# Two value tiles of the 32-wide attentions projected inside heads 2 and 3

## The reference

```
q, k, v = split_heads(src @ w + b)            # 16 heads, 512 tokens, 32 wide
scores = einsum('bhqd,bhkd->bhqk', q, k) / sqrt(32)
scores = scores * mask - 10000.0 * (1.0 - mask)
out = einsum('bhqk,bhkd->bhqd', softmax(scores), v)
```

## Time and profile before

| | |
|---|---|
| median of 3 runs | 4309.42 us (4300.68 to 4310.7) |
| the profiled execution | 4298.77 us |
| its span in the trace | 4296.9 us |
| busy, share of the span | PE 88%, PEld 54%, DVE 61%, ACT 53%, POOL 39% |
| mean granted clock of PE | 0.955 |

### The profile page before, as it was taken

One profiled execution on the slowest core, in us unless ns is written; L12 is line 12 of the kernel. 1 busy time (PEld: TensorE's weight loads), 2 busy tenths in 40 slices (PEclk: granted clock), 3 DMA queues, 4 the chain that ended last, 5 costly groups with the idle time before them and its releaser, 6 DMA issues. The chain is left out here.

```text
span 4296.9 us, 65250 instructions
## 1 busy us (share of the span) xinstructions
PE 3771.7 (88%) x23680; PEld 2331.9 (54%) x23680; DVE 2631.9 (61%) x5803; ACT 2290.6 (53%) x4528; POOL 1696.6 (39%) x1869
## 2 busy tenths in 40 slices
PE   7889899898888989989888898998988898899898
PEld 4544565556544456555654545655555454555555
DVE  5765645656576564665657656466666775646655
ACT  5665734434666573444466657344446575634444
POOL 4544542232454454222245444422224644442222
PEclk9999999899999999989999999999998999999899
DMA  4042220102204221010220322201022132210102
GB/s 134 15 120 55 83 69 31 59 21 99 74 16 120 58 80 69 31 59 25 94 74 22 113 64 74 69 31 59 30 95 71 40 91 65 83 59 31 59 32 97
DMA packets 94554, 276.01 MB, mean 64 GB/s; under 512 B 25472, under 2 KB 25984, under 8 KB 73088
## 3 DMA queue, kind: packets, MB, share of 16 engines
q1 hardware_dynamic: 94208, 271.58, 19.7%
HBM read 201.24 MB, written 4.19 MB: 48 GB/s over the span
## 5 line engine op out<-in xcount | busy, mean ns | idle before, releaser
L806 POOL TENSOR_SCALAR probs<-probs,row_inv 128x512 f32<-128x512 f32 x1024 | 696.0, 697 | 638.8 <-DVE row_inv L721 638.8
L665 ACT ACTIVATE probs<-probs,row_max 128x512 f32<-128x512 f32 x1024 | 733.5, 725 | 130.2 <-DVE row_max L737 128.9
L560 PE MATMUL ps<-ident,probs 128*128 128x128 f32 x4096 | 609.7, 290 | 172.8 <-ACT pT L659 146.3
L560 PEld LDWEIGHTS ps<-ident,probs 128*128 128x128 f32 x4096 | 480.1, 147 | 383.6 <-ACT pT L659 210.1
L659 ACT ACTIVATE pT<-ps 128x512 f32<-128x512 f32 x768 | 430.5, 603 | 112.4 <-PE ps L560 111.5
L370 PE MATMUL ps<-mix,wring 128*128 128x512 f32 x1024 | 471.0, 596 | 3.1 <-DMA wring<-in_blocks_dram 3.1
L535 PE MATMUL ps<-kstack,qstack 96*128 96x512 f32 (+1 forms) x1024 | 381.0, 467 | 15.8 <-DVE row_max L737 6.5
L737 DVE CUSTOM_DVE_ANT_0 probs<-ps,maskA 128x512 f32<-128x512 f32 x512 | 329.2, 681 | 42.5 <-PE ps L535 42.5
L737 DVE CUSTOM_DVE_ANT_0 probs<-ps,neg 128x512 f32<-128x512 f32 x512 | 340.7, 685 | 8.9
L370 PEld LDWEIGHTS ps<-mix,wring 128*128 128x128 f32 x1024 | 191.2, 190 | 198.1 <-issue 178.6
L1550 POOL TENSOR_TENSOR hinv<-hvar,minus_half 128x32 f32<-128x32 f32 x24 | 146.3, 6094 | 284.4 <-DVE hvar L1260 284.4
(11 more groups left out here) (179 smaller groups left out, 7313.7 us busy)
## 6 DMA issues: line engine op xcount, KB each, us to landing
wring<-in_blocks_dram SPq DMA_DIRECT2D x151, 1024.0 KB, 5.1
qstack<-hi SPq DMA_DIRECT2D x256, 64.0 KB, 2.0
kstack<-hi SPq DMA_DIRECT2D x256, 64.0 KB, 2.0
maskA<-in_mask_dram SPq DMA_DIRECT2D x9, 1024.0 KB, 7.5
rows<-in_rows_dram SPq DMA_DIRECT2D x8, 1024.0 KB, 4.7
qstack<-hi SPq DMA_DIRECT2D x256, 32.0 KB, 2.0
qstack<-lo SPq DMA_DIRECT2D x128, 64.0 KB, 2.0
kstack<-lo SPq DMA_DIRECT2D x128, 64.0 KB, 2.0
```

The costliest lines, as they stand in the source:

```text
L560: ins = nc.tensor.transpose(tile[:, qc * P:(qc + 1) * P], probs[:, m % PSLOTS, qc, kc * P:(kc + 1) * P], ident[:, :])
L665: nc.scalar.activation(p, p, ACT.Exp, bias=row_max[:, n % PSLOTS, qc:qc + 1], scale=-1.0, accum_out=row_sum[:, n % PSLOTS, qc:qc + 1]).the ...
L806: nc.gpsimd.tensor_scalar(p, p, row_inv[:, (n - 1) % PSLOTS, qc:qc + 1], 1.0, ALU.mult, ALU.mult)\
```

## The change

The new list `projects` says which half projections stand in which head of attentions 1 and 2. The q and k tiles of groups 2 and 3 stay in heads 0, 1, 4 and 5. Value tiles 2 and 3 leave their place ahead of head 0 and are projected in heads 2 and 3, in two halves of two feature chunks each. DVE empties them after its last maximum of that head. Value tiles 0 and 1 stay ahead of the heads. In attention 2 nothing is left between the q tiles and head 0. `pe_values` becomes `pe_v` for one tile or half of one; attention 0 is computed as before. ACT's and POOL's conditions are written with `projects` and give the same instructions as before.

```diff
-        def to_N(pe, tile, w, src, tc, n=H, base_=0, fin=None, ready=None):
+        def to_N(pe, tile, w, src, tc, n=H, base_=0, fin=None, ready=None, fcs=range(C)):
-            for fc in range(C):
+            for fc in fcs:
...
+            if C - 1 in fcs:
+                m.then_inc(*fin)
...
+                self.projects = {0: ('q', 2), 1: ('k', 2), 2: ('v', 2), 3: ('v', 3), 4: ('q', 3), 5: ('k', 3)}
+                if self.shared:
+                    self.projects = {}
...
+        def pe_v(pe, A, tc, fcs=range(C), tile=None):
+            if tc == 0 and 0 in fcs:
+                w_wait(pe, A.vblk)
+            tile = take(pe, 'v', A.tag, tc) if tile is None else tile
+            to_N(pe, tile, weights(A.vblk), A.src, tc, n=A.vcols, base_=A.voff, fcs=fcs,
+                 fin=tile_ready.reach('v', A.tag, tc) if C - 1 in fcs else None)
+            return tile
...
             if t == 1:
...
                 pe_k(pe, A, 1)
-                pe_values(pe, A)
+                pe_v(pe, A, 0)
+                pe_v(pe, A, 1)
             if t == 2:
                 pe_queries(pe, A)
-                pe_values(pe, A, (2, 3))
...
-                    if not A.shared and g + 2 < A.groups and i < 2:
-                        part = (pe_q, pe_k)[i](pe, A, g + 2, fcs=(2 * half, 2 * half + 1), tile=None if half == 0 else part)
+                    if n in A.projects:
+                        kind, c = A.projects[n]
+                        part = {'q': pe_q, 'k': pe_k, 'v': pe_v}[kind](pe, A, c, fcs=(2 * half, 2 * half + 1),
+                                                                       tile=None if half == 0 else part)
...
         def dve_attention(dve, A):
             t = A.tag
             if t < 2:
-                dve_values(dve, A, range(C))
+                dve_values(dve, A, range(C) if A.shared else range(2))
...
                     if n < A.heads:
                         add_max(n, 2 * half + 1)
+                if A.projects.get(n, 'q')[0] == 'v':
+                    dve_values(dve, A, (A.projects[n][1],))
...
-                    dve_values(dve, A2, range(C))
+                    dve_values(dve, A2, range(2))
```

More of the change, by code:

```diff
@@ L380, in to_N @@
                 m = nc.tensor.matmul(tile[:, 0:n], src[:, fc, tc * P:(tc + 1) * P],
-                                     w[:, fc * H + base_:fc * H + base_ + n], start=(fc == 0), stop=(fc == C - 1))
-            m.then_inc(*fin)
+                                     w[:, fc * H + base_:fc * H + base_ + n], start=(fc == 0), stop=(fc == C - 1),
+                                     skip_group_check=(len(fcs) < C))
+            if C - 1 in fcs:
+                m.then_inc(*fin)
         def dve_stats(dve, tag, tc):
@@ L504, in pe_attention @@
                 pe_queries(pe, A, (0,))
-                pe_values(pe, A)
+                for tc in range(C):
+                    pe_v(pe, A, tc)
                 pe_queries(pe, A, (1, 2, 3))
@@ L675, in act_attention @@
                     nc.scalar.activation(oT[:, c, :], ps[:, OBANK, :], ACT.Copy).then_inc(*act_done.reach('context', t, c))
-                for step in (('x0', 'e0', 'x1', 'e2', 'x2', 'x3') if A.shared else ('e0', 'e1', 'x0', 'x1', 'e2', 'e3', 'x2', 'x3', 's')):
-                    if step == 's' and not A.shared and g + 2 < A.groups and i < 2:
-                        act_split(act, A, 'qk'[i], g + 2)
+                for step in (('x0', 'e0', 'x1', 'e2', 'x2', 'x3', 's') if A.shared else ('e0', 'e1', 'x0', 'x1', 'e2', 'e3', 'x2', 'x3', 's')):
+                    if step == 's' and A.projects.get(n, 'v')[0] != 'v':
+                        act_split(act, A, *A.projects[n])
                     if step[0] == 'e' and 0 <= m < A.heads:
@@ L689, in dve_values @@
             t = A.tag
-            if t < 2:
+            if t < 2 and 0 in tiles:
                 dve.wait_ge(sems['rows_in'], 16 * (t + 1))
@@ L797, in pool_attention @@
                 g, i = divmod(n - 1, 4)
[L798 to L802, removed]
+                if A.projects.get(n - 2, 'v')[0] != 'v':
+                    pool_split(pool, A, *A.projects[n - 2])
                 for qc in range(C):
@@ L1613, in _ @@
                     pe_k(pe, A2, 1)
-                    pe_values(pe, A2, (0, 1))
+                    pe_v(pe, A2, 0)
+                    pe_v(pe, A2, 1)
                     pe_norm_turn(pe, 'ln2', xn)
```

## The result

The changed kernel takes 4347.51 us (median of 4 runs), the kernel before 4308.39: the ratio is 1.0087, with a 95% interval of 1.0072 to 1.0102. It is slower by 0.9%. The forecast was +34 us, the measured difference of the medians +39.

A forecast was written before the change was run, and what follows sets the result against it. DVE's mask and maximum bound the heads, PE only in heads that also project; start gain, clock and stretch sum to +2.35 us in attention 1, +6.2 in attention 2, +34.2 over four samples: 4343 us, range 4317 to 4363.

The forecast's parts named there:

- The start: Ahead of head 0: attention 1 gains 3.35 us (3.0 to 3.8), until its last stack DMA lands; attention 2 gains 0.
- The stretch: Heads 2 to 5: moved value matmuls and evictions delay masks by 4.2 us per attention (bounds 1.2 to 6.7).
- The walk: Step-by-step timing through heads 2 to 5 of attention 1: masks later by 1.4, 2.1, 2.8, 3.5, 4.3 and 4.2 us.
- The clock: After idle PE ahead of head 0, half clock costs 1.5 us in attention 1, 2.0 in attention 2 (bounds 0 to 2.9).
- The third case: Rival: clock falls inside heads 2 and 3 too, about 1.5 us more per attention, +46 us, 4355; chance 0.15.
- The sum: Attention 1 +2.35 us, attention 2 +6.2, so +8.55 per sample and +34.2 in four samples.

The follow-up runs named there:

- The run without the tiles: Kernel before with value tiles 2 and 3 of attentions 1 and 2 not projected, DVE copying tile 0 into them instead: 4287.75 us, ratio 0.9949.
- the run that has nothing else: Kernel before, all value tiles kept ahead of head 0, with value tiles 2 and 3 projected a second time in heads 2 and 3: 4343.99 us, ratio 1.0094.
- the run in the context's bank: Changed kernel with value tiles 2 and 3 in the context's bank, free until head 6, instead of a ring bank: 4317.19 us, ratio 1.0017.
- The fill: Changed kernel with unread matmuls in the idle places ahead of head 0 (8 instructions in attention 1, 16 in attention 2): 4303.81 us, ratio 0.9992.
- the shifted kernel: Kernel before with 12 unread one-column matmuls (48 instructions) ahead of the transposes of layer 1's first norm: 4281.67 us, ratio 0.9945.
- the shifted changed kernel: Changed kernel with 12 unread one-column matmuls (48 instructions) ahead of the transposes of layer 1's first norm: 4312.61 us, ratio 1.0018.
- one tile in quarters: Kernel before with only attention 1's value tile 3 moved, projected by quarters in heads 2 and 3 into the context's bank: 4295.21 us, ratio 0.9977.

## Why the prediction was right

*The start.* Right. "PE starts it at 253.07, straight behind the 13.9 us of value matmuls", while the stack would have let it start at 250.4: the start of attention 1 gained 3.2 us (forecast 3.35) and was ended by a kstack<-lo DMA, that of attention 2 gained nothing and was ended by a qstack<-hi DMA. The run without the tiles shows it from the other side: taking 53 us of matmuls away gave 18.5, only about 3 of it in the attentions.

*The stretch.* Right in size: 4.4 us in the run that has nothing else, forecast 4.2. The walk was right step by step too, within 0.2 us at each mask. It did not say how much of the sum hung on the ring; the run in the context's bank does: about 2.5 of 4.4 us.

*The clock.* Right at the starts. In attention 2 the first mask came 0.4 later and the second another 1.6 (4.1 instead of 2.5 from mask to mask), 2.0 in all, as forecast; in attention 1 it was 1.0 to 1.3, forecast 1.5. The third case, the clock falling inside head 2, came true in four of eight attentions (13.99 us from head 2 to head 4 without it, 15.65 with it), +6.6 us that the sum did not hold. The measured time lies between the forecast and that case, so its closeness to the forecast is in part luck. The profile after was to show 4 to 6 us more from head 0 to head 7; in attention 2 it was 7.3 for this reason. The fill shows that idle PE is the cause: it takes 16 of these 17.5 us back from head 0 to head 7.

*The sum.* -13 (start of attention 1), +1.5 (first masks of attention 2), +35 (stretch), and +17.5 for the clock after the first mask (11 at the starts, 6.6 in head 2) make +41. The forecast had -13.4, +33.6 and +14. It missed the falls in head 2, and was a little high at the start of attention 1.

*What it did not see.* The stalls of the recurrent layers. They number 7 before and 8 after, so they hardly enter the comparison, one stall and the clock behind it being some 3 us (688.60 to 691.73 is 3.1 us where the shifted kernel has 1.8, and 1.5 us of stall). This too was luck: moving the tiles leaves the number of PE instructions per sample as it was but for one. Had the change added 48 ahead of the stalls, the result would have been some 35 us lower (4312.61 in the shifted changed kernel), in large part for a reason that no reading of the attentions would find. That the profiled execution differed by 8 us more than the attentions explain is in part the eighth stall; the rest stays open.

## What to carry to other kernels

Before moving work out of a start-up, ask what the stage waits for next: here a chain of small DMAs ended the wait in one attention and stood 3 us behind in the other, so taking away both tiles was worth 3.2 us in the one and nothing in the other. Work put into a pipelined loop costs by the order and the buffers it passes through: the same matmuls cost 4.4 us through a ring of three banks and 1.9 through a free bank, and one tile in quarters cost 0.5. When a change adds or removes instructions on a long stream, compare stages that it doesn't touch, and run a control with harmless instructions in the same place, before believing a difference of half a per cent. The control can change more than it is meant to, so compare its stages too: here it also kept the clock up at the start of attention 1.

## What the runs showed of the hardware

Bursts of 128 small matmuls (1.8 us for 128) stalled for 1.0 to 1.9 us in the kernel before, once in each pass of a recurrent layer, in 7 of 8 passes. 48 instructions ahead removed all stalls, the same 48 behind none; 25 us of 4307 hung on that. In 13 traces all 62 such stalls stand at places of PE's stream that are a multiple of 256 instructions apart, to within one. This fits a fetch of instructions in blocks that comes late when a block is used up fast. The Trainium skill (Runtime: NRT & Kernel Launch, section "Instruction fetch mechanics") says that each engine's instructions are fetched in blocks of 256 while the one before executes, and that this stays mostly hidden. The traces agree with the 256. They don't show the fetch itself, and if it is the cause, it was not hidden here.

The granted clock fell behind idle stretches of very different length: 8.4 us, 3.5 us, and in the filled kernel 1.74 and 1.90 us, while it stayed up behind 2.3 us in all four samples of the shifted changed kernel. So the length of the last idle stretch alone doesn't tell whether it falls. The price depended on what stood behind: 1.1 us where two halves of a head ran at 1.2 GHz for part of the time, 2.0 where head 0 did for the whole of it, and nothing for most of the later falls, which DVE's pace covered: in the kernel before the mean clock around heads 2 and 3 was 0.75 to 0.87 in five attentions and 1.00 in three, and from head 2 to head 4 all eight took 10.35 or 10.36 us.
